# A graph-attention layer on one core: chunks 2 to 7 of x centred before they are turned, and the first stage in a new order

## What is computed

```python
h = jnp.maximum(_layernorm(x, axis=-1), 0.0)
x = x + _L0_gnn_ref(h, adj, W, b_W, a_vec, b_a)

# _L0_gnn_ref(node_features, adjacency_matrix, W, b_W, a_vec, b_a):
h = node_features @ W.T + b_W
a1, a2 = (a_vec[:D_OUT], a_vec[D_OUT:])
e = (h @ a1)[:, None] + (h @ a2)[None, :] + b_a[0]
e = jnp.where(e > 0, e, 0.2 * e)
scores = jnp.where(adjacency_matrix > 0, e, jnp.float32(NEG_INF))
attention = jax.nn.softmax(scores, axis=1)
h_prime = attention @ h
```

## Time and profile before

| | us |
|---|---|
| median of 3 runs | 209.23 |
| lowest and highest | 208.92, 209.34 |
| the profiled execution | 209.82 |
| its span, first to last instruction | 208.2 |

### The profile page before, as it was taken

The page is one execution under the profiler, slowest core; times in us unless marked ns, Lnnn a source line. Parts: engine busy times, 40 slices in busy tenths (PEclk is TensorE's granted clock), DMA queues, the critical chain, the costliest instruction groups (busy, mean ns, idle before and its releaser), DMA issues.

```text
span 208.2 us, 7164 instructions
## 1 busy us (share of the span) xinstructions
PE 198.0 (95%) x3176; PEld 191.8 (92%) x3176; DVE 183.3 (88%) x268; ACT 141.4 (68%) x129; POOL 47.5 (23%) x65
## 2 busy tenths in 40 slices
PE   0998999999999999999999999999999999999993
PEld 0686789899999999999999999999999999999992
DVE  3828997999999999987999998979998899989753
ACT  2388866997671777779775766798677737987000
POOL 1052879899950020440000000000000000000000
PEclk9999999999999999999999999999999999999999
DMA  5999999999999999999999999999999999980321
GB/s 180 352 416 406 404 402 410 404 404 404 413 422 405 409 408 408 405 411 408 406 407 408 390 391 416 409 407 408 410 407 406 378 416 409 411 336 37 104 66 40
DMA packets 24160, 75.66 MB, mean 363 GB/s; under 512 B 1600, under 2 KB 5952, under 8 KB 24000
## 3 DMA queue, kind: packets, MB, share of 16 engines
q1 hardware_dynamic: 23984, 75.06, 91.7%
q10 hardware_dynamic: 144, 0.13, 0.3%
HBM read 73.08 MB, written 2.11 MB: 361 GB/s over the span
## 4 chain that ended last, share of the span: by engine, by line
issue 60%; DMA 14%; PE 12%; ACT 5%; DVE 4%; POOL 3%; SPq 1%; POOLq 0%
DMA adj_sb<-in_adj_t 12%; ACT mask L380 5%; PE ps L752 3%; PE ps L762 3%; DMA wp<-in_w_pack 2%; DVE w L452 2%; PE ps L784 1%; PE ps L786 1%; PE ps L790 1%; SPq L313 1%; POOL tx L733 1%; POOL bad L738 1%; POOL tt L735 1%; POOL bad L737 1%; DVE stats L523 1%
## 5 line engine op out<-in xcount | busy, mean ns | idle before, releaser
L784 PE MATMUL ps<-V,w 128*128 128x129 f16 x1024 | 177.3, 219 | 0.7 <-DVE V L566 0.3
L786 PE MATMUL ps<-V,w 128*128 128x129 f16 x1024 | 177.3, 223 | 0.0
L790 PE MATMUL ps<-V,w 128*128 128x129 f16 x1024 | 177.3, 218 | 0.0
L380 ACT ACTIVATE mask<-adj_sb 128x2048 bf16<-128x2048 int32 x62 | 117.7, 1914 | 37.7 <-DMA adj_sb<-in_adj_t 31.5
L452 DVE SCALAR_TENSOR_TENSOR w<-g_row,pairs,mask 128x1024 f32<-128x1024 f32 x96 | 117.8, 1280 | 8.1 <-ACT mask L380 5.2
L790 PEld LDWEIGHTS ps<-V,w 128*128 128x128 f16 x1024 | 102.0, 100 | 0.0
L784 PEld LDWEIGHTS ps<-V,w 128*128 128x128 f16 x1024 | 99.2, 97 | 2.3 <-issue 1.2
L786 PEld LDWEIGHTS ps<-V,w 128*128 128x128 f16 x1024 | 99.8, 97 | 0.6 <-issue 0.6
L452 DVE SCALAR_TENSOR_TENSOR w<-ps,pairs,mask 128x1024 f32<-128x1024 f32 x32 | 38.7, 1275 | 0.4 <-issue 0.4
L742 POOL PARTITION_ALL_REDUCE bad<-bad x1 | 0.4, 380 | 114.7 <-DVE bad L505 114.7
L762 PEld LDWEIGHTS ps<-wp,hT 128*128 128x128 f32 x64 | 8.9, 209 | 2.0 <-issue 1.5
(11 more groups left out here) (87 smaller groups left out, 59.3 us busy)
## 6 DMA issues: line engine op xcount, KB each, us to landing
adj_sb<-in_adj_t SPq DMA_DIRECT2D x64, 1024.0 KB, 11.1
xT<-in_x_t SPq DMA_DIRECT2D x8, 256.0 KB, 7.5
x_sb<-in_x_p SPq DMA_DIRECT2D x3, 512.0 KB, 10.9
g_row<-g_dram SPq DMA_DIRECT2D x1, 1536.0 KB, 10.6
out<-xT SPq DMA_DIRECT2D x3, 512.0 KB, 11.8
x_sb<-in_x_p SPq DMA_DIRECT2D x2, 256.0 KB, 4.2
out<-xT SPq DMA_DIRECT2D x1, 192.0 KB, 2.1
out<-xT SPq DMA_DIRECT2D x3, 64.0 KB, 1.5
```

Of the source, the lines that this page charges most:

```text
L380: nc.scalar.activation(mask[:, m % MASKS, :], adj_sb[:, m % HELD, :], ACT.Relu, scale=CONNECTED).then_inc(mask_ready, 1)
L784: nc.tensor.matmul(sums[:, bank, a, :], w16[:, m % SLOTS, col:col + P, 1], V[:, jt, 0:NF], start=(jt == 0 and a == 0), stop=False, skip_gr ...
L786: nc.tensor.matmul(sums[:, bank, a, :], w16[:, m % SLOTS, col:col + P, 1], V[:, jt, NF:2 * NF], start=False, stop=False, skip_group_check= ...
L790: last = nc.tensor.matmul(sums[:, bank, a, :], w16[:, m % SLOTS, col:col + P, 0], V[:, jt, 0:NF], start=False, stop=(jt == NT - 1), skip_g ...
```

## The change

**Loads.** Only chunks 0 and 1 of `xT` are still loaded; the six transfers of 256 KB for chunks 2 to 7 are gone. `load_xt(1)` now stands ahead of the two first loads of `x_sb`, and `load_x(3)`, `load_x(4)` follow the first adjacency loads.

**Centring and turning.** For chunks 2 to 7 `centre_x` takes the mean away from `x_sb`, on POOL for chunks 2 to 5 and on DVE for 6 and 7, into `xc`, which is the memory of `xT`. `turn_chunk` on PE turns the four tiles of a chunk with four transposes by `ident`, in place of `centre_chunk`. The spreading of the maximum and of the factors is done by transposes too.

**PE.** Eight products of `ones` with `ones` go ahead of everything. Of the chunks only 0, 1, 2 and the turning of 3 stand ahead of the first step; `h_chunk(3)` to `h_chunk(7)` and `turn_chunk(4)` to `turn_chunk(7)` stand between steps 0 and 6. Step 0 may start when a quarter of its weights is there (`w_begun`).

**ACT, DVE and POOL.** `highs` on ACT now writes V straight from H with four scaled copies, and DVE makes `prod`. Mask 0 is made half by DVE and half by ACT (`first_mask`), mask 1 by ACT. `weigh(0, 0)` is cut in two (`weigh_first`). `statistics(2)` is cut in two around the reciprocals. `scores(1)` moves behind `weigh(2, 0)`, `scores(2)` behind `weigh(7, 1)`. POOL makes the deviations of sets 3 and 4 (tiles 16 to 31) in one go behind `halves(3)`, and `add_b` goes behind all `halves`. At the end `check_sums` comes after the last `rows`.

The order on PE from the product that follows the norm to the first step. First before: `xT,centre` is `centre_chunk`, `wp,hT` is `h_chunk`, `ident,tt` and `ident,pairs` are the spreading.

The diff, cut to what matters (the declarations, `X_BANK` and `H_BANK`, the waits of step 0 on PE and renumbered waits are left out):

```diff
...
-    EARLY = 2
+    EARLY = 1
+    WARM = 8
...
                 load_xt(0)
+                load_xt(1)
                 load_x(0)
                 load_x(1)
-                load_xt(1)
                 load_x(2)
-                load_xt(2)
-                load_xt(3)
                 load_adj(0)
-                load_xt(4)
+                load_x(3)
                 load_adj(1)
-                load_xt(5)
-                load_x(3)
+                load_x(4)
                 load_adj(2)
-                load_xt(6)
-                load_x(4)
-                load_xt(7)
                 load_adj(3)
...
-                def products(c):
+                def highs(c):
                     act.wait_ge(scaled_ready, 1)
                     act.wait_ge(ones_ready, 1)
                     act.wait_ge(h_ready, c + 1)
                     for j in range(CT):
                         g = c * CT + j
-                        ins = nc.scalar.activation(prod[:, c % 2, j, :], H[:, g, H0:HC], ACT.Copy,
-                                                   scale=evr[:, g:g + 1])
-                    ins.then_inc(product_ready, 1)
-                def highs(c):
-                    act.wait_ge(product_ready, c + 1)
-                    nc.scalar.activation(V[:, c * CT:(c + 1) * CT, 0:NF], prod[:, c % 2, :, :],
-                                         ACT.Copy).then_inc(high_ready, 1)
+                        ins = nc.scalar.activation(V[:, g, 0:NF], H[:, g, H0:HC], ACT.Copy, scale=evr[:, g:g + 1])
+                    ins.then_inc(high_ready, 1)
...
+                def first_mask():
+                    act.wait_ge(adj_loaded[0], 16)
+                    nc.scalar.activation(mask[:, 0, GC:2 * GC], adj_sb[:, 0, GC:2 * GC], ACT.Relu,
+                                         scale=CONNECTED).then_inc(mask_first, 1)
...
+                relu_chunk(0)
+                relu_chunk(1)
                 roots_part()
-                relu_chunk(1)
+                take_chunk(0)
+                take_chunk(1)
                 nc.scalar.activation(warm[:], zero_col[:], ACT.Exp)
-                take_chunk(0)
+                weights(0)
                 relu_chunk(2)
-                take_chunk(1)
+                first_mask()
+                highs(0)
+                take_chunk(2)
                 relu_chunk(3)
-                take_chunk(2)
-                weights(0)
+                mask_part(1)
+                highs(1)
                 take_chunk(3)
+                mask_part(2)
+                mask_part(3)
                 relu_chunk(4)
-                products(0)
-                highs(0)
                 weights(1)
+                mask_part(4)
                 take_chunk(4)
                 relu_chunk(5)
-                products(1)
-                highs(1)
-                mask_part(2)
+                mask_part(5)
                 take_chunk(5)
                 relu_chunk(6)
-                mask_part(3)
+                mask_part(6)
                 take_chunk(6)
                 relu_chunk(7)
-                mask_part(4)
+                mask_part(7)
                 take_chunk(7)
-                mask_part(5)
                 weights(2)
...
+                def weigh_first(half):
+                    r = slice(half * GC // 2, (half + 1) * GC // 2)
+                    dve.wait_ge(mask_early, 1)
+                    dve.wait_ge(rows_spread, half + 1)
+                    nc.vector.scalar_tensor_tensor(w[:, 0, r], g_ps[:, r], pairs[:, 1, 0:1], mask[:, 0, r], ALU.max,
+                                                   ALU.min).then_inc(w_begun if half == 0 else w_ready, 1)
...
+                def centre_x(i):
...
+                    dve.wait_ge(stats_ready, i - FIRST_SETS + 1)
+                    nc.vector.tensor_tensor(mean[:, r], stats[:, r, 1], stats[:, r, 4], ALU.add).then_inc(mean_ready, 1)
+                    dve.wait_ge(mean_ready, 1)
+                    for g in range(*SETS[i], CT):
+                        nc.vector.scalar_tensor_tensor(
+                            xc[:, g:g + CT, :],
+                            mean[:, g:g + CT].rearrange("p (n a) -> p n a", a=1).to_broadcast([P, CT, DIN]), -0.5,
+                            x_sb[:, g:g + CT, :], ALU.mult, ALU.add).then_inc(x_centred_last, 1)
...
+                def products(c):
+                    r = slice(c * CT, (c + 1) * CT)
+                    dve.wait_ge(scaled_ready, 1)
+                    dve.wait_ge(ones_ready, 1)
+                    dve.wait_ge(h_ready, c + 1)
+                    nc.vector.tensor_tensor(prod[:, c % 2, :, :], H[:, r, H0:HC],
+                                            evr[:, r].rearrange("p (n a) -> p n a", a=1).to_broadcast([P, CT, NF]),
+                                            ALU.mult).then_inc(product_ready, 1)
                 def lows(c):
+                    dve.wait_ge(product_ready, c + 1)
...
+                statistics(2, 0, 4)
...
-                statistics(2)
+                statistics(2, 4, 8)
...
-                early_mask(0)
+                early_mask()
                 pack(0)
                 scale_weights(0)
+                products(0)
+                dve.wait_ge(pairs_ready, 1)
+                weigh_first(0)
+                lows(0)
+                weigh_first(1)
+                weigh(0, 1)
+                statistics(3)
+                weigh(1, 0)
+                weigh(1, 1)
+                products(1)
+                lows(1)
+                weigh(2, 0)
                 scores(1)
-                statistics(3)
-                dve.wait_ge(pairs_ready, 1)
-                dve.wait_ge(rows_spread, 2)
-                weigh(0, 0)
-                lows(0)
-                weigh(0, 1)
-                early_mask(1)
+                weigh(2, 1)
+                weigh(3, 0)
                 pack(1)
                 scale_weights(1)
-                weigh(1, 0)
-                lows(1)
-                weigh(1, 1)
+                weigh(3, 1)
                 dve.wait_ge(pairs_ready, 2)
                 statistics(4)
-                weigh(2, 0)
-                weigh(2, 1)
-                weigh(3, 0)
-                weigh(3, 1)
-                scores(2)
+                centre_x(4)
                 weigh(4, 0)
                 weigh(4, 1)
+                weigh(5, 0)
+                weigh(5, 1)
+                weigh(6, 0)
+                weigh(6, 1)
+                weigh(7, 0)
+                weigh(7, 1)
+                scores(2)
                 pack(2)
                 scale_weights(2)
                 dve.wait_ge(pairs_ready, 3)
                 nc.vector.transpose(gT[:], pairs[:, 0, :]).then_inc(gT_ready, 1)
-                for m in range(5, NM):
+                for m in range(8, NM):
...
-                    if i == len(PIECES) - 1:
-                        check_sums()
                     rows(i)
+                check_sums()
...
+                def centre_x(i):
...
+                    pool.wait_ge(stats_ready, i - FIRST_SETS + 1)
+                    step(nc.gpsimd.tensor_tensor(mean[:, r], stats[:, r, 1], stats[:, r, 4], ALU.add))
+                    step(nc.gpsimd.tensor_scalar(mean[:, r], mean[:, r], 0.5, None, ALU.mult))
+                    for g in range(*SETS[i], CT):
+                        nc.gpsimd.tensor_tensor(xc[:, g:g + CT, :], x_sb[:, g:g + CT, :],
+                                                mean[:, g:g + CT].rearrange("p (n a) -> p n a", a=1).to_broadcast([P, CT, DIN]),
+                                                ALU.subtract).then_inc(x_centred, 1)
...
-                deviations(2)
-                deviations(3)
+                centre_x(2)
+                deviations(2, 3)
+                centre_x(3)
                 halves(2)
-                deviations(4)
                 halves(3)
+                deviations(3, 5)
+                halves(4)
+                halves(5)
+                halves(6)
+                halves(7)
                 add_b(0)
                 add_b(1)
...
+                def turn_chunk(c):
+                    if c < 6:
+                        pe.wait_ge(x_centred, c - 1)
+                    else:
+                        pe.wait_ge(x_centred_last, c - 5)
+                    pe.wait_ge(relu_ready, c)
+                    for j in range(CT):
+                        last = nc.tensor.transpose(ps[:, X_BANK[c], j * P:(j + 1) * P], xc[:, c * CT + j, :], ident[:])
+                    last.then_inc(centred, 1)
...
+                pe.wait_ge(ones_set, 1)
+                for _ in range(WARM):
+                    nc.tensor.matmul(ps[:, 7, 0:P], ones[:], ones[:], start=True, stop=True)
...
-                centre_chunk(2)
                 h_chunk(1)
-                centre_chunk(3)
-                h_chunk(2)
                 pe.wait_ge(t_limits, 1)
...
-                h_chunk(3)
-                centre_chunk(4)
```

(26 more changed lines are left out.)

67 lines of the change are left out of this document (37 added, 30 removed).

## The result

The changed kernel takes 213.62 us (median of four executions, 212.81 to 215.01), the kernel before 209.07 us on the same chip: 1.0215 times as long, 95% interval 1.0179 to 1.0251. The forecast was 211.0, from 208.8 to 213.2. So the direction was right, but the time lies 0.4 us above the range: the loss is 4.5 us where 1.75 was worked out.

The account below looks back on a forecast made before the run. PE alone was taken to bound the kernel from step 5, so step 8's start decides: 1.4 us later there plus 0.3 at the end gives +1.7 on the span; for the median 209.23 + 1.75 = 211.0 us, range 208.8 to 213.2.

Parts of the forecast that it names:

- The start of step 0: First product of the second stage on PE: at 19.2 us against 22.23 before, 3.0 earlier.
- rival (1): PE's clock falls to half speed ahead of step 0, among gaps and transposes: +2.0 us, 213.0; chance 0.17.
- From step 0 to step 4: DVE sets the pace; step 4 starts at 36.3 against 38.0 before, 1.7 of the 3.0 us left.
- 0.15 + 1.3: DVE's time for `centre_x(4)` before step 4: mean 0.15 us, twice 512 columns 1.3 us.
- From step 4 to step 8: PE waits 1.35 us at step 8 for V of chunk 4; step 8 starts at 51.0, 1.4 later than before.
- The end: Behind the last product: `check_sums` after the last `rows` and all engines reading `flag` cost +0.3 us.
- (2): Each transpose on PE takes two records, not one: +1.4 us, 212.4; chance 0.13.
- (4): Waits before step 4 and at step 8 don't bind; PE starts step 8 at 47.7: 207.6 us; chance 0.12.
- The sum: Whole kernel: 1.4 + 0.3 = +1.7 us on the span; median 209.23 + 1.75 = 211.0 us.
- "Adjacency comes early enough": From step 5 on, adjacency loads don't hold up PE, so the 1.5 MB of `xT` no longer loaded is worth nothing.

Follow-up runs that it names:

- few_wide: pool_waits plus five products of ones of 512 columns on PE ahead of step 0; 211.88 us, ratio 1.0102 to the kernel before.
- pool_waits: The changed kernel with one more wait: POOL starts `halves(3)` only when DVE has centred the last set; 212.02 us, ratio 1.0131 to the kernel before.
- stream: few_wide with ACT's masks 7 and 8 moved ahead of its takes of chunks 6 and 7; 209.68 us, ratio 1.0051 to the kernel before.
- mended: stream with chunks 4 and 5 as own part, `deviations(3, 5)` ahead of `halves(3)` replacing POOL's wait, flag's sums before last rows; 211.83 us, ratio 1.0159.

## Why the prediction was wrong in its size

**The start of step 0** (forecast 19.2, measured 19.84). Two errors partly cancel. POOL started at 12.22 and took 1.24 for the first centring, not 1.5, so it was done at 14.1 and not at 14.9. A transpose is one record, as taken. But rival (1) came true here: the granted clock was 0.50 from 13 to 19 us, the four transposes of `turn_chunk(2)` took 1.11 in place of 0.60 and `h_chunk(2)` 1.80 in place of 1.06. I had priced this at 1.1 us by step 0, which few_wide's start at 17.73 against 19.23 makes 1.5. Its effect on the end, which I had put at 2.0 us, was 1.2 at step 4 and still 1.2 at step 8 in the traces of few_wide and pool_waits; 0.8 of that was lost again in the waits for weights near 197 us, so 0.4 reached the last product. The Trainium skill, page "TensorE: Matmul & The Clock Gate", Part 4: PE-mode transpose, says that transposes don't count as PE activity and that full speed does not engage for them. No run here shows whether it was that or the idle time around them, since few_wide filled both; transposes do run faster at the upper level, 0.23 and 0.11 us each.

**From step 0 to step 4** (36.3, measured 38.42). This step failed. Its term for `centre_x(4)`, 0.15 + 1.3, measured 3.5. The 1.3 is right to the hundredth for DVE alone (pool_waits), and 0.15 + 1.3 became 3.5 because `halves(3)` and the end of `halves(2)` stood beside it. I had named that interference one step earlier, from the lengths of L686, and had applied it to POOL only, and to the centring on POOL only. The forecast never asked what POOL does while DVE centres. Its rows would have told: at 3.23 us a chunk from `scale_weights(1)` on, POOL is at `halves(2)` and `halves(3)` just then. The reading of L686 was also too coarse. DVE worked beside the fast one of 1.67 as well (29.57 to 34.41), only at weights that read `ps`; so what counts is which instruction stands beside it. And the length of the 128x32 instruction of `scores(2)`, 0.62 in the earlier trace rows, held this interference already. Before, POOL was busy beside it; in the changed kernel POOL is idle there:

```profile
35.51 1.14 POOL L715 TENSOR_TENSOR V<-prod,V 128x516 f16<-128x516 f32 x1
...
49.41 0.13 DVE L570 TENSOR_TENSOR st<-H,rstd 128x32 f32<-128x32 f32 x1
```

The same thing made the half mask and L578 long ahead of step 0:

```profile
13.02 1.44 DVE L477 TENSOR_SCALAR mask<-adj_sb 128x1024 bf16<-128x1024 int32 x1
14.38 1.01 DVE L578 TENSOR_SCALAR bounded<-eg 128x16 f32<-128x16 f32 x1
...
29.98 0.16 DVE L578 TENSOR_SCALAR bounded<-eg 128x16 f32<-128x16 f32 x1
```

(the first two beside POOL's centring, the third with POOL quiet). It was not everything on DVE that grew beside POOL. The centring, with two inputs in SBUF, did; the weights, whose main input is `ps`, kept their 1.21 a half; and the statistics, with one input in SBUF, took 1.63 for eight beside `halves(2)` (31.83) and 1.65 with POOL quiet. Nor is it always DVE that pays. In the kernel before, the low part of V kept its length and POOL's product beside it took 1.61 in place of 1.05:

```profile
26.22 0.68 DVE L566 TENSOR_TENSOR V<-prod,V 128x516 f16<-128x516 f32 x1
...
26.20 1.61 POOL L714 TENSOR_TENSOR prod<-H,evr 128x516 f32<-128x516 f32 x1
```

The Trainium skill, page "GPSIMD Engine Reference", the table ahead of section 1.1 Terminology, names VectorE instructions with two SBUF inputs or in a two-port mode as those that contend with GpSimd. The centring (1.47 for 0.65), the weights (1.21) and the statistics (1.63) agree with it.

**From step 4 to step 8** (14.7 us, measured 15.9). The wait for V of chunk 4 came where it was forecast, 0.9 us longer than a step from start to start, and not 1.35. The chain from `h_chunk(7)` to V was 6.3 us and not 6.8, since that instruction of `scores(2)` took 0.13 and not 0.62. What is missing is the second fall of the clock: step 4 took 3.99 us and not 2.77, and `h_chunk(6)` 0.4 more than at full clock. These 1.6 less the 0.5 of the chain are the 1.2 us, within 0.1; they are there in the profiled execution and probably in one other. The sum had this term at nothing, and no rival had it: I looked for gaps on PE ahead of step 0, and had myself forecast waits of 1.9 us between step 0 and step 4 without asking what the clock would make of them.

**The end** (+0.3): +0.38 between the last product and the flag, as forecast. Of the other rivals, a transpose in two records (2) is refuted by the records, and PE did wait ahead of step 4 and step 8, against (4).

**The sum.** At step 8 the trace is 3.3 us behind the forecast: 2.1 up to step 4 and 1.2 from there. In the ratios, 1.3% or 2.7 us are left of the 4.5 with the interference and, in its trace, the second fall gone (pool_waits, 2.1 to 3.4 by its interval), and 1.0% or 2.1 us with the early clock kept as well (few_wide, 1.1 to 3.2). The forecast's 1.75, whose sum had none of the three, lies within the second and just below the first. How the rest divides between the interference and the second fall is known in the traces only.

**"Adjacency comes early enough"** held for the changed kernel, whose other losses hid it, and would have failed for a faster one: few_wide pays 1.3 us, 150 us later, for the gap in the transfers at 42 to 50 us, as stream shows. The 0.5 us of pool_waits stand at the same place, but were not tried by themselves.

## What to carry to other kernels

Moving an elementwise operation between VectorE and GpSimd is priced by what the other engine does in those microseconds: read both timelines side by side at the new place. Where two instructions overlap, of which the one on VectorE was of a kind that grew here, take as bounds the plain length and that length plus one instruction of the other engine; the most that was added here was 0.95 us on VectorE, beside instructions of 1.05 to 1.14 (an estimate for others, from these lengths). A wait that the sum forecasts on TensorE has to be asked what it does to the clock of the step behind it, and an engine that works in order and holds back a stream of transfers (ScalarE in its takes) has to be asked what it delays far behind. When several waits are taken away at once, the freed engines move beside new neighbours, so look at the trace again after each.

## What was not expected of the hardware

- GpSimd and VectorE slow each other: 512 columns centred on VectorE took 0.65 us alone and 1.47 beside GpSimd, whose 1.05 and 1.14 became 1.50 and 1.46. Instructions of 16 columns on VectorE went from 0.12 to 0.17 up to 0.96 to 1.12, but not all of them: a cast beside GpSimd kept its 0.18 in mended (47.90). Statistics and weights kept their lengths too.
- The end of the program grew by 3.0 to 3.4 us, from 2.2 or 2.3 behind the flag to 5.2 to 5.6, in the traces of the three kernels with 3226 or more matmul records of PE, and in none with 3207 or fewer, in the changed and in the old kernel alike. PE's branch took 3.5 to 3.9 us there and 0.48 before. What lies between, and whether it is the count or the place of the code behind it, wasn't tried.
- In one trace the granted clock fell 1.3 us after PE had taken up its products again behind 2.1 us of idle time, and stayed at half for 3.4 us with PE busy. With six short products in the idle time it stayed up in the one trace there is, and by the means in the other executions too.
- A float32 product of one column took 0.21 us a record, two records to a product, at the start of the program, where one of 128 columns took 0.24 (3.78 us for 16 records). At the upper level of the clock it wasn't measured.
